# Two perceiver cross-attention stages of one kernel, rebuilt with keys on the partitions and the maximum taken off before the exponential

## What is computed

```python
qn = layernorm(x, ln_q_g, ln_q_b)
q  = qn @ Wq * 64 ** -0.5                 # 16 heads of 64
k, v = split(media @ Wkv, 2)              # media: 8 x 1601 keys x 128 channels
sim  = where(media_mask, q @ k.T, neg_inf)   # per head 256 x 1601
attn = softmax(sim, axis=-1)
x = x + tanh(attn_gate) * ((attn @ v) @ Wo)
h = layernorm(x, ln_ff_g, ln_ff_b)
x = x + tanh(ff_gate) * (gelu(h @ W1) @ W2)
```

## Time and profile before

| what | value |
|---|---|
| time, median of 3 runs (lowest, highest) | 5918.71 us (5918.25, 5936.94) |
| profiled execution, its time | 5930.45 us |
| its span, first to last instruction | 5928.7 us |
| mean granted clock of PE | 0.953 of full speed |
| busy share of the span: PE, DVE, ACT, POOL | 91%, 49%, 46%, 14% |
| attention of L0, where it lies in the span | 58 to 1824 us |
| attention of L3, where it lies | 4021 to 5790 us |

### The profile page before, as it was taken

One profiled execution on the slowest core, in us unless ns is written; L12 is line 12 of the kernel. 1 busy time (PEld: TensorE's weight loads), 2 busy tenths in 40 slices (PEclk: granted clock), 3 DMA queues, 4 the chain that ended last, 5 costly groups with the idle time before them and its releaser, 6 DMA issues. The chain is left out here.

```text
span 5928.7 us, 105399 instructions
## 1 busy us (share of the span) xinstructions
PE 5422.6 (91%) x37144; PEld 4315.0 (73%) x37144; DVE 2898.4 (49%) x4864; ACT 2744.9 (46%) x5391; POOL 826.1 (14%) x1101
## 2 busy tenths in 40 slices
PE   7999999999998799698988869858999999999997
PEld 6888888888886577455555559547888888888886
DVE  3444444444444343566566646234444444444444
ACT  4554554554553355345455520335554454554552
POOL 1111111111101122111111032001111111111101
PEclk9999999999998899789899979878999999999998
DMA  1000000000000000222222100210000000000000
GB/s 50 8 1 8 8 1 8 8 1 8 1 1 15 24 0 0 45 39 36 37 42 37 27 31 0 81 38 15 8 1 9 8 1 9 8 1 8 1 1 29
DMA packets 36812, 97.40 MB, mean 16 GB/s; under 512 B 12576, under 2 KB 24096, under 8 KB 35232
## 3 DMA queue, kind: packets, MB, share of 16 engines
q1 hardware_dynamic: 36384, 91.71, 6.9%
HBM read 59.04 MB, written 2.10 MB: 10 GB/s over the span
## 5 line engine op out<-in xcount | busy, mean ns | idle before, releaser
L976 DVE CUSTOM_DVE_ANT_0 L_attn_probs<-L_attn_ps_s,L_attn_bias 128x1608 f32<-128x1608 f32 x512 | 938.5, 1833 | 945.7 <-PE L_attn_ps_t L839 936.5
L1076 ACT ACTIVATE L_attn_pT<-L_attn_ps_t 128x512 f32<-128x512 f32 (+1 forms) x1536 | 746.1, 486 | 1240.2 <-PE L_attn_ps_t L839 1240.2
L839 PE MATMUL L_attn_ps_t<-ident,L_attn_probs 128*128 128x128 f32 (+1 forms) x6656 | 1010.6, 278 | 18.5 <-DVE L_attn_v_sb L988 7.3
L839 PEld LDWEIGHTS L_attn_ps_t<-ident,L_attn_probs 128*128 128x128 f32 (+1 forms) x6656 | 753.0, 140 | 217.7 <-issue 136.2
L1099 ACT ACTIVATE L_attn_probs<-L_attn_probs,L_attn_negmax 128x1601 f32<-128x1601 f32 x512 | 832.0, 1625 | 2.9 <-DVE L_attn_negmax L976 2.8
L863 PE MATMUL L_attn_ps_u<-L_attn_pT,L_attn_v_sb 128*64 128x256 f32 (+1 forms) x6656 | 830.5, 387 | 0.0
L1626 ACT ACTIVATE L_cross_probsT<-L_cross_ps_st 128x512 f32<-128x512 f32 (+1 forms) x832 | 482.9, 597 | 471.2 <-PE L_cross_ps_st L1352 452.5
L863 PEld LDWEIGHTS L_attn_ps_u<-L_attn_pT,L_attn_v_sb 128*64 128x64 f32 (+1 forms) x6656 | 433.1, 136 | 244.3 <-issue 45.8
L1512 DVE TENSOR_REDUCE L_cross_part<-L_cross_ps_s 128x1 f32<-128x804 f32 x512 | 500.9, 993 | 185.8 <-PE L_cross_ps_s L1339 183.1
L822 PE MATMUL L_attn_ps_s<-L_attn_ctx_hi,L_attn_g_hi 128*128 128x402 f32 x2048 | 511.6, 372 | 38.8 <-issue 32.3
L822 PE MATMUL L_attn_ps_s<-L_attn_ctx_lo,L_attn_g_hi 128*128 128x402 f32 x2048 | 468.7, 351 | 0.0
(11 more groups left out here) (275 smaller groups left out, 8378.9 us busy)
## 6 DMA issues: line engine op xcount, KB each, us to landing
L_cross_kx<-A SPq DMA_DIRECT2D x256, 100.5 KB, 2.8
L_attn_ctx_in<-in_ctxT SPq DMA_DIRECT2D x16, 804.0 KB, 4.4
memory_ctx<-in_ctx SPq DMA_DIRECT2D x8, 832.0 KB, 5.9
Bw<-in_ctxT SPq DMA_DIRECT2D x8, 804.0 KB, 4.4
memory_ctxT<-in_ctxT SPq DMA_DIRECT2D x8, 804.0 KB, 4.4
...
```

Of the source, the lines that this page charges most:

```text
L839: ins = pe.transpose(ps_t[g % 2][0:w, (k % 4) * P:(k % 4 + 1) * P], source[:, k * P:k * P + w], st.ident[:, :])
L976: dve.tensor_tensor_reduce(out=by_chunk(probs[qt]), in0=by_bank(ps_s), in1=by_chunk(bias), scale=-1.0, scalar=BIG, op0=ALU.add, op1=ALU.mi ...
L1076: act.activation(pT[j % 2][s // 2][0:w, tiles[0]:tiles[-1] + 1, s % 2 * P:(s % 2 + 1) * P], ps_t[g % 2][0:w, 0:P * len(tiles)].rearrange(" ...
```

## The change

The group's work is done the other way round. Scores have keys on partitions from the start: for each of 13 tiles of 128 keys, three matmuls give 128 keys x 512 columns (two heads of 256 queries) in one of four PSUM banks. In this layout the mask is a bias per partition, so the copy out of PSUM, now by ACT, adds it (`take_scores`). The probabilities are then already as `pv` needs them: `turn`, `take_probs`, `pT` and the class `TurnFills` go. But the maximum over keys is now one over 13 tiles and 128 partitions. DVE takes the maximum over tiles in three `tensor_reduce` (`running_max`, the first over 6 tiles, then over 4 and 3, each with the result before in one more row), PE turns the 128 x 512 result (`turn_tops`), DVE reduces it to one number a column (`highest`), PE spreads these over all partitions (`spread_tops`), and DVE subtracts them from the scores in place in three pieces (`shift`). ACT applies the exponential in place in three pieces. The sums over keys, before a by-product of ACT, are made by POOL over tiles (`add_up`) and by PE over partitions (`take_sums`).

```diff
+    GROUPS = [range(0, 6), range(6, 10), range(10, KT)]
+    SLOTS = KT + 2
+    def at(k):
+        return k + (k >= 6) + (k >= 10)
...
-        probs = [ph.sb(f"probs{i}", [P, S_EVEN]) for i in range(2)]
-        pT = [[ph.sb(f"pT{i}{k}", [P, KT, Q]) for k in range(HG)] for i in range(2)]
+        probs = [ph.sb(f"probs{i}", [P, SLOTS, W]) for i in range(2)]
-        ps_s = ph.ps("ps_s", [P, 4 * BANK])
-        ps_t = [ph.ps(f"ps_t{i}", [P, BANK]) for i in range(2)]
+        ps_s = [ph.ps(f"ps_s{i}", [P, BANK]) for i in range(4)]
+        ps_x = ph.ps("ps_x", [P, BANK])
+        ps_v = ph.ps("ps_v", [P, BANK])
...
+            def add_up(J, j, first):
...
+                pool.tensor_tensor(both, p[:, at(0):at(0) + 2, :], p[:, at(2):at(2) + 2, :], ALU.add).then_inc(added_up, 1)
+                for n, k in enumerate(range(4, 12, 2)):
...
+                    pool.tensor_tensor(both, both, p[:, at(k):at(k) + 2, :], ALU.add).then_inc(added_up, 1)
...
+            def scores(j, k):
+                keys = slice(k * P, (k + 1) * P)
+                out = ps_s[(KT * j + k) % 4][:, :]
+                pe.matmul(out, ctx_hi[:, keys], g_hi[:, :], start=True, stop=False)
+                pe.matmul(out, ctx_hi[:, keys], g_lo[:, :], start=False, stop=False)
+                pe.matmul(out, ctx_lo[:, keys], g_hi[:, :], start=False, stop=True).then_inc(scored, 1)
...
+            def turn_tops(J):
+                pe.wait_ge(maxed, NG * (J + 1))
+                for t in range(4):
+                    ins = pe.transpose(ps_x[:, t * P:(t + 1) * P], high[:, t * P:(t + 1) * P], st.ident[:, :])
+                ins.then_inc(turned, 1)
+
+            def spread_tops(J):
+                pe.wait_ge(tops_ready, J + 1)
+                for t in range(4):
+                    ins = pe.matmul(ps_x[:, t * P:(t + 1) * P], tops[:, t:t + 1].to_broadcast([P, P]), ident_r[:, :],
+                                    start=True, stop=True)
+                ins.then_inc(m_ready, 1)
...
+            def running_max(J, j, n):
+                tiles = GROUPS[n]
+                source = slice(at(tiles[0]) - (n > 0), at(tiles[-1]) + 1)
+                out = high[:, :] if n == NG - 1 else probs[j % 2][:, at(tiles[-1]) + 1, :]
+                dve.wait_ge(taken, KT * J + tiles[-1] + 1)
...
+                dve.tensor_reduce(out, probs[j % 2][:, source, :].rearrange("p k q -> p q k"), AX_X, ALU.max).then_inc(maxed, 1)
+
+            def highest(J):
+                dve.wait_ge(turned, J + 1)
+                dve.tensor_reduce(tops[:, :], ps_x[:, :].rearrange("p (t k) -> p t k", k=P), AX_X, ALU.max).then_inc(tops_ready, 1)
+
+            def shift(J, j, n):
+                tiles = GROUPS[n]
+                s = probs[j % 2][:, at(tiles[0]):at(tiles[-1]) + 1, :]
...
+                dve.tensor_tensor(s, s, ps_x[:, :].unsqueeze(1).to_broadcast([P, count, W]), ALU.subtract).then_inc(shifted, 1)
...
+            def take_scores(b, J, j, k):
+                act.wait_ge(scored, KT * J + k + 1)
+                act.activation(probs[j % 2][:, at(k), :], ps_s[(KT * j + k) % 4][:, :], ACT.Identity,
+                               bias=bias_now[:, k:k + 1]).then_inc(taken, 1)
+
+            def exponential(J, j, n):
+                s = probs[j % 2][:, at(GROUPS[n][0]):at(GROUPS[n][-1]) + 1, :]
+                act.wait_ge(shifted, NG * J + n + 1)
+                act.activation(s, s, ACT.Exp).then_inc(exped, 1)
```

More of the change, by code:

```diff
@@ L858, in pv @@
+                    ins = pe.matmul(out, ctx_lo[:, c], wv_hi[i % 2][:, :], start=False, stop=True)
+                ins.then_inc(v_made, 1)
+            def pv(j, run):
                 v = v_sb[j // 2 % 2]
-                for k in PV_TILES[part]:
+                for k in PV_RUNS[run]:
                     w = min(P, S - k * P)
@@ L960, in _ @@
+            pe.wait_ge(consts_ready, 2)
+            make_g(0, 0, 0)
+            drive(pe, slot)
+            J = J_ALL
+            spread_inverse(J - 2)
             output(J - 2, NJ - 2)
-            for part in range(len(PV_TILES)):
-                wait_turned(rnd, part, 0, "over")
-                pv(NJ - 1, part)
+            pe.wait_ge(exped, NG * J)
+            for run in range(2):
+                pv(NJ - 1, run)
             pe.wait_ge(x_added, J - 1)
+            take_sums(J - 1, NJ - 1)
@@ L1133, in _ @@
             context_high(0)
-            g_high(0, 0)
-            drive(act, batch)
-            for g, s in ((3, 0), (0, 0), (2, 0), (3, 1)):
-                take_probs(J_ALL // 2, g, 0, s, "over")
+            g_high(0)
+            drive(act, slot)
+            copy_inverse(J_ALL - 2)
             copy_inverse(J_ALL - 1)
```

604 lines of the change are left out of this document (277 added, 327 removed).

## The result

The changed kernel takes 6890.18 us, median of 4 runs (6886.52 to 6897.37), beside 5927.82 us of before in the same session: a ratio of 1.161 (95% interval 1.156 to 1.165). The forecast was 7000 us, its own range 6520 to 7150.

A forecast was written before the change was run, and what follows sets the result against it. PE's instructions bound the kernel at 27.29 us a group; a cross-engine chain of 18.0 + 15.2 (reductions) + 2.5 (slow clock) = 35.7 us would, over 128 groups, add 1077: 7000 us, own range 6520 to 7150, overall 5790 to 7250.

The forecast's parts named there:

- R: DVE's three reductions, 7680 elements read at a 2048-byte stride: 1.92 ns an element, 15.2 us a group.
- 12 ns on 16 elements: Extra time of a small DVE addition reading words 24 bytes apart, taken as 1.76 ns an element against 1.04.
- POOL's clearing row: POOL clearing words 36 bytes apart, 2.1 times the contiguous cost; gave the upper rate, 2.08 ns an element for DVE.
- B: Rival: strided reads cost DVE's reductions nothing, R 8.5 us, chain 26.5 us a group, 5815 us; chance 0.29.
- D: Rival: half the stride surcharge, reductions at 1.40 ns an element, R 11.2 us, 6160 to 6480 us; chance 0.10.
- C: Rival: 2.5 ns a word or a cost per short result, R 19.7 us, 40.2 us a group, 7570 us; chance 0.07.
- Step 4: Turn, column maximum and spread, with `make_g` ahead of the spread: 2.9 us, plus 2.5 at PE's half clock.
- Step 2: ACT's six score copies, with `copy_inverse` between and a hand-over, until the first reduction starts: 4.6 us.
- steps 1 and 5: Tail of ACT's exponentials behind the last subtraction, 2.0 us; DVE's three subtractions with `g_low` between, 8.1 us.
- What was costed at nothing: POOL's sums (14.6 us and 3 of splits), ACT's work (about 18), mask loads: hidden; fill and drain near 5 and 20.

The follow-up runs named there:

- e8: Kernel with the column maximum taken straight from PSUM, PE's turning, next g and spread moved ahead of the first half of `pv`: 5714.43 us, ratio 0.964.
- e1: Changed kernel with the three reductions reading the same 7680 elements in the order they lie, exponential scaled by 0: 6030.89 us.
- e4: Changed kernel with `make_g` moved from ahead of `spread_tops` to behind it: 6745.18 us.
- e3: Changed kernel with 26 extra PE matmuls of 512 columns, result unread, just ahead of `turn_tops`: 6776.28 us.
- e7: Changed kernel with pairwise maxima on contiguous rows for the reductions, and POOL's four additions of 1024 left out: 5989.64 us.

## Why the prediction was right

**The question was the right one.** PE's own work was put at 23.4 us a group; e8, where little else holds it up, shows 23.6. So removing 52 turns did make room for a gain of some 500 us, and in the changed kernel the chain across the engines took it, and more.

**R decided, by the stride.** The step from 12 ns on 16 elements to 1.76 ns an element was right in kind: the mean of the three reductions is 1.76. That it holds to the second digit is luck. 12 / 16 is 0.75 and not 0.72 ns, which would make 1.79; the 12 ns come from a handful of small operations; and the three reductions run at 1.83, 1.73 and 1.69. What failed was the next step, the middle between this and twice the contiguous rate: POOL's clearing row was the wrong neighbour, and R was 14.0 instead of 15.2 us, 1.2 x 128 = 154 us too much. The reductions' rows rule out B (1.04 ns), D (1.40) and C (2.5); C's other ground, a cost of each short result, fell with e1.

**Step 4 was right in kind.** PE waited 732.0 / 128 = 5.7 us for the reductions (7 forecast), the clock went to 0.50 behind it, and `make_g` stood on the chain (e4). It cost 4.5 us in the group shown, not 5.4. e3 says which term was too large: without the slow clock the step takes 2.8 us (2.9 priced), so the slow clock cost 1.5 us in the mean and not 2.5.

**Step 2 was sized too small, for two hold-ups not seen.** The price of six copies took their scores as ready. All but the first tile stand behind `spread_inverse`, which waits for DVE's last instruction of the slot, and the sixth behind `output` as well; the order of the code on PE has both, and the prediction read that order only at the end of the slot. It cost 1.3 us in the group shown and 1.6 in the mean, and by luck it offset the excess in R and in step 4: by the table 1.1 us each, with 0.3 each in steps 1 and 5. So the sum of 35.7 us missed 34.6 by less than its parts did.

**What was costed at nothing** held in most groups: POOL's sums, ACT's other work and the mask loads are in nobody's wait there. Once a batch POOL holds up DVE's copy of the mask numbers for 2.2 us, as shown under e7. At a stage's end POOL is in the chain: the last group's sums keep DVE waiting 10 us in the drain.

```profile
2289.05 0.18 DVE L954 RECIPROCAL L_attn_inv<-L_attn_ps_m 128x4 f32<-128x4 f32 x1 [10.09 <-PE L_attn_ps_m L835]
```

From the first score to the last addition of the first stage lie 2230 us, before 1759; 63 times 7.3 explains 460 of these 471, so fill and drain grew by some 11 us a stage, not by none. The two stages make up 931 of the 967 us between the two profiles; the rest lies between them, mostly in the narrow stage (1004 against 975 us).
